# From the last state of the selective scan to the first expert tile: another order of the two batches, and the last state's output on VectorE

## The reference

```python
# two Mamba blocks; the last one's end, per batch b:
h = dA * h + v;  y_t = einsum('ben,bn->be', h, C_t)      # 16 states n
y = ys + dp * xb
y = y * silu(z)                                          # the gate
x = x + ga * einsum('ble,de->bld', y, ow)                # out product, added to x
# then the mixture of experts
h = layernorm(x) * (1 + cb) + sb
xn = layernorm(h) * ln_gamma + ln_beta
logits = xn @ router_w                                   # 8 experts, top 2
...
out = sum over e of comb[:, e] * swiglu(xn, gate_up_w[e], down_w[e])
out = out + swiglu(xn, shared_gate_up_w, shared_down_w)  # the shared expert
```

## Time and profile before

| | |
|---|---|
| time, median of 3 runs | 1183.24 us (1182.34 to 1191.7) |
| the profiled execution | 1189.21 us, its span 1187.8 us |
| TensorE, VectorE busy | 1061.5 us (89%), 1001.9 us (84%) |
| ScalarE, GpSimd busy | 819.6 us (69%), 573.1 us (48%) |
| granted TensorE clock, mean | 0.935 |

### The profile page before, as it was taken

How to read it: one execution, slowest core, us unless ns; L and a number is a source line. 1 busy time by engine, 2 the same in 40 slices (tenths; PEclk the granted TensorE clock), 3 DMA queues, 4 the chain that set the end, 5 groups by cost and what they waited for, 6 DMA issues and landing times. The chain is left out here.

```text
span 1187.8 us, 21214 instructions
## 1 busy us (share of the span) xinstructions
PE 1061.5 (89%) x7811; PEld 663.6 (56%) x7811; DVE 1001.9 (84%) x1333; ACT 819.6 (69%) x1623; POOL 573.1 (48%) x457
## 2 busy tenths in 40 slices
PE   6899999999999869899999989899999977499982
PEld 4222222223223244478888874488878864398882
DVE  5899989999994688889999977899999986667664
ACT  3289888999998537977877827988877813355551
POOL 5401340000011120159999970199998974355653
PEclk9789999999999888899999999899999986699996
DMA  5110101000000500112222200112222209111114
GB/s 158 61 42 15 29 15 29 15 29 16 15 2 20 142 19 3 56 39 104 90 88 91 90 18 3 56 54 90 90 88 90 89 19 276 17 37 39 41 42 118
DMA packets 45990, 69.31 MB, mean 58 GB/s; under 512 B 14030, under 2 KB 27342, under 8 KB 45888
## 3 DMA queue, kind: packets, MB, share of 16 engines
q1 hardware_dynamic: 40152, 60.62, 16.4%
q0 software_dynamic: 2496, 5.14, 1.7%
q10 hardware_dynamic: 3240, 2.20, 0.7%
HBM read 55.47 MB, written 9.13 MB: 54 GB/s over the span
## 5 line engine op out<-in xcount | busy, mean ns | idle before, releaser
L2166 PEld LDWEIGHTS m_pair<-filter_w,delta_x_t 128*128 128x128 f32 x2560 | 296.5, 193 | 36.4 <-issue 33.5
L532 DVE TENSOR_REDUCE neg_max<-max_ps 128x1 f32<-128x1024 f32 x256 | 295.9, 1215 | 17.3 <-PE max_ps L521 17.1
L2166 PE MATMUL m_pair<-filter_w,delta_x_t 128*128 128x112 f32 (+3 forms) x2560 | 300.0, 276 | 11.0 <-DVE m_pair L2176 5.0
L648 ACT ACTIVATE exp_scores<-score_k 128x512 f32<-128x512 f32 x512 | 270.9, 605 | 29.7 <-PE score_k L640 24.0
L2145 ACT ACTIVATE decay<-delta,a_log 128x1024 f32<-128x1024 f32 x128 | 145.9, 1143 | 75.1 <-DVE normed L2176 36.2
L521 PE MATMUL max_ps<-k_rows,q_rows 48*128 48x512 bf16 x512 | 164.6, 404 | 12.1 <-DVE neg_max L532 10.3
L2137 ACT ACTIVATE filter_w<-filter,b_t 128x112 f32<-128x112 f32 (+1 forms) x576 | 167.5, 376 | 0.0
L640 PE MATMUL score_k<-q_rows,k_rows 51*128 51x512 bf16 x512 | 164.0, 392 | 2.4 <-ACT exp_scores L648 0.6
L667 PE MATMUL av_ps<-exp_scores,v_cols 128*32 128x256 f32 x2048 | 158.4, 394 | 0.0
L2176 DVE TENSOR_TENSOR_SCAN m_pair<-decay,m_pair 128x1024 f32<-128x1024 f32 x64 | 145.9, 2279 | 1.7 <-PE m_pair L2166 1.4
L541 POOL CAST neg_max_parts<-neg_max 128x16 bf16<-128x16 f32 x16 | 3.2, 198 | 237.5 <-DVE neg_max L532 237.5
(11 more groups left out here) (314 smaller groups left out, 1542.2 us busy)
## 6 DMA issues: line engine op xcount, KB each, us to landing
c_row<-c_rows SPq DMA_DIRECT2D x64, 512.0 KB, 3.6
gate_up_all<-in_gate_up_w SPq DMA_DIRECT2D x8, 512.0 KB, 7.2
qk_parts<-part SPq DMA_DIRECT2D x12, 256.0 KB, 2.8
delta<-h_t SPq DMA_DIRECT2D x24, 128.0 KB, 2.3
q_rows<-qk_parts SPq DMA_DIRECT2D x91, 32.0 KB
down_all<-in_down_w SPq DMA_DIRECT2D x8, 256.0 KB, 7.8
moe_normed<-normed SPq DMA_DIRECT2D x4, 512.0 KB, 11.7
k_rows<-qk_parts SPq DMA_DIRECT2D x15, 96.0 KB
```

What stands on the lines that cost most here:

```text
L532: ve.tensor_reduce(nm[leg % 2][:, 4 * j + qt:4 * j + qt + 1], mps[:, bank:bank + 2, :].rearrange("p a q -> p (a q)"), AX_X, ALU.max, negat ...
L648: ac.activation(pt[a % 4][:, HEADS[r % 4], :], eps[:, bank, :], ACT.Exp, scale=SC).then_inc(*exped.up())
L2166: mm = pe.matmul(vps[blk][:, lo:hi], self.duT[b][:, c, blk * P:(blk + 1) * P], wf[g % 3][:, lo:hi], start=True, stop=True)
```

## The change

1. The last state of the last layer's second batch: its block 1 is multiplied and added on VectorE (`ve_last`) and no longer on GpSimd. Its add waits for GpSimd's add of the state before.
2. Both gates of batch 1 are made right behind it, before anything else of the end of `mamba`. The out products of both batches follow each other on TensorE.
3. `mamba` adds both batches to X and takes both statistics, and then centres, shifts and measures batch 0 and batch 1; nothing of that is left in `experts`.
4. In `experts` the two batches are normalised, turned and multiplied with the router's weights with nothing of the shared expert between them. GpSimd's constants come right behind the roots.
5. Only `shared_up(0)` stands ahead of the counts. The other three, all four silus and all four hidden products follow behind `ve_places` in program order.

```diff
--- before.py
+++ after.py
@@ -1365,8 +1365,8 @@
         self.s_w, self.s_v, self.s_decay, self.s_hs = (
             self.sig(n) for n in ("filter_w", "v_mm", "decay", "h_scan"))
         self.s_ys, self.s_ysum, self.s_gated = (self.sig(n) for n in ("y_mul", "y_sum", "y_gated"))
-        self.s_yg, self.s_yacc, self.s_skip, self.s_pair = (
-            self.sig(n) for n in ("y_mul_g", "y_add_g", "skip_g", "y_pair"))
+        self.s_yg, self.s_yacc, self.s_skip, self.s_pair, self.s_last = (
+            self.sig(n) for n in ("y_mul_g", "y_add_g", "skip_g", "y_pair", "y_last"))
         self.c_in = [self.sig(f"c_in{k}") for k in range(3)]
         self.shifted, self.roots, self.rms, self.rms_normed = {}, {}, {}, {}
 
@@ -1413,21 +1413,24 @@
             y_ready = self.mamba_scan(l, in_w_all, y_ready)
 
 
-
         self.ring.bind(halves[4:], first=4)
+        gated = [y_ready[0](), y_ready[1]()]
         for engine in (pe, ve):
             engine.wait_ge(*self.inputs_gated)
-        out = self.pe_out(NL - 1, 0, y_ready[0](), (self.s_hs.sem, self.s_hs.n - 1))
+        out = self.pe_out(NL - 1, 0, gated[0], (self.s_hs.sem, self.s_hs.n - 1))
+        out.update(self.pe_out(NL - 1, 1, gated[1], self.s_hs.at()))
         added = [self.ve_out(self.X, c, out[c]) for c in (0, 1)]
-        root = self.ln_root(self.X, 0, TB, added)
-        for t in range(TB):
-            self.ve_center(t, 1, 3)
-        out.update(self.pe_out(NL - 1, 1, y_ready[1](), self.s_hs.at()))
-        shifted = [self.ve_shift(self.N, t, 1, 3, root) for t in range(TB)]
-        self.norm_roots = [self.ln_root(self.N, 0, TB, shifted[-1:])]
-        added = [self.ve_out(self.X, c, out[c]) for c in (2, 3)]
-        self.x_root = self.ln_root(self.X, TB, NT, added)
-        self.mamba_read, self.out_read = out[3].full, added
+        roots = [self.ln_root(self.X, 0, TB, added)]
+        added += [self.ve_out(self.X, c, out[c]) for c in (2, 3)]
+        roots.append(self.ln_root(self.X, TB, NT, added[2:]))
+        self.norm_roots = []
+        for b in range(NB):
+            ts = range(b * TB, (b + 1) * TB)
+            for t in ts:
+                self.ve_center(t, 1, 3)
+            shifted = [self.ve_shift(self.N, t, 1, 3, roots[b]) for t in ts]
+            self.norm_roots.append(self.ln_root(self.N, b * TB, (b + 1) * TB, shifted[-1:]))
+        self.mamba_read, self.out_read = out[3].full, added[2:]
 
     def ve_mamba_center(self, b):
         for t in range(b * TB, (b + 1) * TB):
@@ -2226,8 +2229,19 @@
             if (b, n) == states[-1]:
                 pe_sum(k, (ys.sem, state(b, n) + 1), True)
 
+        def ve_last(b, n):
+
+            g, step = state(b, n), self.s_last
+            h = hh[g % 2]
+            for m in ((c_in[g % 3].sem, 16 * (g // 3 + 1)), (hs.sem, NBLK * g + 2), added.at()):
+                ve.wait_ge(*m)
+            ve.tensor_tensor(h, h, csb[g % 3][:], ALU.mult).then_inc(*step.up())
+            ve.wait_ge(*step.at())
+            ve.tensor_tensor(yacc[b], yacc[b], h, ALU.add).then_inc(*step.up())
+
         def ve_gate(b, blk):
-            ve.wait_ge(*(ysum.at(), (added.sem, state(b, DS - 1) + 1))[blk])
+            ended = self.s_last.at() if (l, b) == (NL - 1, NB - 1) else (added.sem, state(b, DS - 1) + 1)
+            ve.wait_ge(*(ysum.at(), ended)[blk])
             y = (yps[:], yacc[b])[blk]
             ve.tensor_tensor(zs[:, blk, b, :], zs[:, blk, b, :], y, ALU.mult).then_inc(*gated.up())
             return gated.at()
@@ -2255,7 +2269,10 @@
                 first_done = ve_gate(b - 1, 1)
             if kind(b, n) == 2:
                 po_pair(b, n)
-            po_output(b, n)
+            if g + 1 < len(states) or l < NL - 1:
+                po_output(b, n)
+            else:
+                ve_last(b, n)
             pe_sums(b, n)
             if g + 1 < len(states):
                 pe_momentum(*states[g + 1], 1)
@@ -2597,36 +2614,28 @@
             def turn(c):
                 self.turn(normed, lambda b: gam[:], lambda b: bet[:], done=ht, chunks=(c,), by=(0, 0, 0, 0))
 
+
+
             shared_in = {}
-            logits = ring.take()
+            logits = [ring.take() for b in range(NB)]
             apply_norm(0, self.norm_roots[0])
             put_normed(0)
-            for t in range(TB, NT):
-                self.ve_center(t, 1, 3)
-            for c in (0, 1):
-                turn(c)
-                pe_logits(c, logits)
-            shifted = [self.ve_shift(self.N, t, 1, 3, self.x_root) for t in range(TB, NT)]
-            root = self.ln_root(self.N, TB, NT, shifted[-1:])
             po_constants()
+            turn(0)
+            turn(1)
+            pe_logits(0, logits[0])
+            apply_norm(1, self.norm_roots[1])
+            put_normed(1)
+            turn(2)
+            pe_logits(1, logits[0])
+            turn(3)
+            pe_logits(2, logits[1])
+            pe_logits(3, logits[1])
+            ruled = ve_constants()
             shared_up(0)
-            shared_up(1)
-            ve_top(0, logits)
-            ruled = ve_constants()
-            apply_norm(1, root)
-            put_normed(1)
-            logits = ring.take()
-            for c in (2, 3):
-                turn(c)
-                pe_logits(c, logits)
-            for c in (0, 1):
-                ac_shared_silu(c)
-                po.wait_ge(*shared_in[c])
-                po_shared_hidden(c)
-            ve_top(1, logits)
+            for b in range(NB):
+                ve_top(b, logits[b])
             masks = ve_masks()
-            shared_up(2)
-            shared_up(3)
             ac_second()
             bank = ring.take()
             pe_counts(masks, bank)
@@ -2634,7 +2643,9 @@
             sp_weights()
             ve_places(bank)
             counted = bank.left
-            for c in (2, 3):
+            for c in range(1, NC):
+                shared_up(c)
+            for c in range(NC):
                 ac_shared_silu(c)
                 po.wait_ge(*shared_in[c])
                 po_shared_hidden(c)
```

## The result

The changed kernel takes 1180.67 us in the median of 16 runs (1176.09 to 1190.09), the kernel before 1187.15 in as many (1179.97 to 1198.68). The ratio is 0.9944, with a 95% interval of 0.9916 to 0.9972: 0.56% faster, some 6.6 us. Timed again in five rounds beside one of the experiments it gave 1178.83 against 1189.58, ratio 0.9928 (0.9893 to 0.9963). The forecast gain was 3.05 us. The forecast time of 1180.2 lies within 0.5 us of the measured 1180.67, but that is luck: it was counted from 1183.24, the median of three runs, while the median of 16 runs of the same kernel is 3.9 us higher, and the gain came out 3.4 us larger.

What follows compares the result with a forecast made beforehand. No single engine bounds the stretch from scans to first expert tile; a chain through TensorE, VectorE and ScalarE does. 6.3 + 1.75 - 0.5 - 4.5 = 3.05 us earlier, from 1183.24 to 1180.2; range 1172 to 1187.5.

Steps and rivals of the forecast that it cites:

- The end of the scans: Both gates through on VectorE at 970.3; batch 1's output product then at full clock, 3.73 us, bounds 3.73 and 6.63.
- Rival C: TensorE's clock falls in the 0.9 us gap before batch 1's output product; 2.5 us lost, 1182.7; chance 0.10.
- The router: Both batches' turns and logits on TensorE, 7.8 us at half clock; logits done at 1003.8 against 1006.9, gain 3.1.
- The exponential: Routing on ScalarE: table load ends at 1009.1, exponential 0.2 later; places begin at 1009.9 against 1016.25, gain so far 6.3.
- The places and one-hots: On VectorE: places gain 1.75 us, clips cost 0.5, hidden products meeting the one-hots cost 4.5 (bounds 0 and 5.0).
- Rival A: GpSimd's hidden products miss VectorE's one-hots; first tile 7.55 us earlier, 1175.7; chance 0.25.
- Rival B: GpSimd's clips over places and first one-hot block VectorE in full, up to 5.85 us, not 0.5; 1185.5; chance 0.12.
- Behind the one-hots: From the one-hots' end to the first tile nothing changes, 7.7 us; the gather hides the shared expert's down products.
- rival D: Expert loop falls into another rhythm, some 2 us either way; chance 0.08 together with something unseen.

Runs made afterwards that it cites:

- The forced silu: Changed kernel plus one unused single-column silu on ScalarE before the first shared product, so the exponential loads its table again; first tile_t at 71.44 against 69.5 us.
- the held-back products: Changed kernel with GpSimd's four hidden products held until the last one-hot is written; one-hots took 8.24 us, first tile_t at 68.39 against 69.5.
- the one with products between the batches: Changed kernel with shared products of chunks 0 and 1 back between the two batches' logits; logits read at 45.62, first tile_t at 75.53 us.

## Why the prediction was right, and where its size was off

The direction, the places of gain and loss and the reason of the loss held; the sum was 3.05, and the stretch gave 5.84 between the first two profiles and 5.4 in the mean of three.

The end of the scans. Forecast: last gate 7.5 behind the scan's start, out product of 3.73 at full clock. Measured: 7.35 and 3.81. Rival C (the clock falls in the gap) did not come true at 0.76 us. At 2.16 the product took 5.44, so the bound was a real one.

The router. Forecast: logits read 41.0 behind the scan's start; measured 39.4. This term was mis-sized by 1.6. I added up the durations of the rows, 1.09 for a turn and 1.88 for a chunk of logits, though groups on TensorE start 0.88 and 1.73 apart: the longer figure holds the tail of the last matmul, which overlaps the next group. From the third turn to the logits' reading it was 6.8 and not 7.8. The other 0.6 lie ahead of the third turn, and no run tells their cause.

The exponential. Forecast: a table load of 1.28 in front of it. This step failed: I saw that a load went but took it for the one before the first silu. In truth two of the three went. With no silu ahead, the exponential found its table; its last use before was in the decays of the scans. The forced silu put the 1.3 us back. Up to the places 6.3 were forecast and 8.96 measured. The router's 1.6 and the load's 1.28 make 2.9, which is more than the difference of 2.66: without the load the places would by my sum have begun 4.8 behind the logits, and they began 5.02 behind them.

The places and one-hots. Forecast: 1.75 gained, 0.5 lost to clips, 4.5 lost to the mutual wait. Measured: 1.80 gained in the places, with clips over them, then 4.26 lost to the mutual wait by the held-back products and 0.29 in one_hot_tile, which stayed at 1.75 us there too and ended with the third clip. Rival A (the products miss the one-hots) is out; its condition, half clock in the twelve records behind the counts, did not come true. Rival B (clips block in full) is out as well. On the rule of the Trainium skill ("SBUF — State Buffer", "Who interferes with whom") the runs agree for GpSimd's two-input products against VectorE's two-input operations. Two one-input operations waited for such products as well, row_from (1.24) and tile_end (1.16) of the run with the products held back. For the clips the runs show waits of at most 0.44 us on single operations, not whole clips, so there the measurement differs from the rule.

Behind the one-hots I took the way to the tile as unchanged: 8.10 against 7.73. But I named the gather as what hides the down products, and this was wrong in both kernels. Before, ScalarE's weights copy, which waits for the expert numbers, and its four copies of the down products behind it release the tile:

```profile
1034.99 1.06 ACT L2682 ACTIVATE gate_up<-gate_up_all 128x1024 f32 x1 [16.98 <-issue]
1035.95 2.04 ACT L2593 ACTIVATE moe_shared<-moe_ps 128x512 f32<-128x512 f32 x4
```

In the changed kernel the last copy waits for the down products themselves, which took 6.34 us there and 4.85 before:

```profile
1040.46 0.60 ACT L2610 ACTIVATE moe_shared<-moe_ps 128x512 f32<-128x512 f32 x1 [0.19 <-PE moe_ps L2605]
```

So behind the one-hots the down products and ScalarE's copies of them were the next limit already.

The expert loop (rival D). Its rest is 139 to 150 us whatever the kernel. In the five longer profiles of both kernels and of the one with products between the batches ScalarE's tile_out waits for a release from outside the program's engines, which its program makes the landing of a scatter three tiles back; in the short ones it does not. ScalarE's waits in the first and in the second profile of the changed kernel:

```profile
ACT tile_out L2740 <- remote: 3.7, 5, 1.2
...
ACT tile_out L2740 <- PE down_ps L2732: 1.8, 3, 0.6
```

```profile
ACT tile_out L2740 <- PE down_ps L2732: 1.7, 1, 1.7
```

Where the loop is long it was 149.6 and 147.6 before against 145.5 and 145.5 after. That may be a second, smaller gain; with the 5.4 of the stretch it would make the 8.5 us of the ratio 0.9928. Two profiles of each don't show it, and it stays open, as does what makes the loop long.

## What to carry to other kernels

Before moving an engine's work out of a critical stretch, ask which of its operations meet which of the other engine's at the new place: GpSimd products and VectorE operations on SBUF add up, and four products of 1.24 us gave back 4.3 of 10.8 us here. When a wait of that kind is removed, follow what starts late instead: twice 4.3 us of waits went and the first tile came only 1.1 and 0.8 us earlier. It gained 4.9 when the consumer (the down products) was fed first and its copies went first on ScalarE. On ScalarE look for the last function used before each table load; here, taking the silus out from ahead of the exponential saved two loads of three.

## What was not expected of the hardware

The kernel before differs by 3.6 us from run to run in this stretch alone (72.9 to 76.5); the rows above show TensorE's clock rising at different moments behind the same idle time of 6.6 us. The changed kernel, with a gap of 0.72 to 0.76, repeats within 0.1. A larger part of the spread between runs lies elsewhere: the last scan starts between 958.4 and 975.3. In the first and third profile of the kernel before, where it starts at 962.8 and 975.3, the granted clock over 340 to 440 us is 0.96 and 0.80 (columns as in the earlier trace rows):

```profile
340.00:440.00 100.00, 84.69 (x571) 31.61 (x569) 71.96 (x187) 65.00 (x118) 16.81 (x23) 0.96 0.21 54
```

```profile
340.00:440.00 100.00, 91.39 (x517) 29.79 (x509) 61.38 (x153) 60.01 (x110) 13.84 (x21) 0.80 0.22 54
```

What brings the clock down there no run tells. One profile of each kernel would have shown a gain of 0.7 us, or of 4.9 in the second pair; the marks within the stretch were needed to read it.
